# Attention and mixture-of-experts layer on one core: first-stage pairs, late rankings and the last output step moved in a slot schedule

## What is computed

```python
x = x + _layernorm(_L0_attn_ref(_layernorm(x), Wq, Wk, Wv, Wo))
x = x + _layernorm(_L0_ffn_ref(_layernorm(x), router_weight, router_bias, gate_up_proj, ...))

score = einsum('bhnd,bhmd->bhnm', q, k) / sqrt(16)      # causal mask, softmax
out = einsum('bhnm,bhmd->bhnd', softmax(score), v)      # then times Wo

topk_w, topk_idx = top_k(softmax(flat @ router_weight.T + router_bias), 2)
gu = flat @ gate_up_proj[e] + gate_up_bias[e]           # 512 gate and 512 up columns
act = (clip(up) + 1) * gate * sigmoid(1.702 * gate)
down = act @ down_proj[e] + down_bias[e]                # summed over the 2 experts by topk_w
```

## Time and profile before

| | us |
|---|---|
| median of three executions | 2084.46 (2081.51 to 2085.91) |
| the profiled execution's own time | 2083.6 |
| its span, first to last instruction | 2081.9 |

### The profile page before, as it was taken

One profiled execution on the slowest core, in us unless ns is written; L12 is line 12 of the kernel. 1 busy time (PEld: TensorE's weight loads), 2 busy tenths in 40 slices (PEclk: granted clock), 3 DMA queues, 4 the chain that ended last, 5 costly groups with the idle time before them and its releaser, 6 DMA issues.

```text
span 2081.9 us, 50245 instructions
## 1 busy us (share of the span) xinstructions
PE 1954.1 (94%) x13588; PEld 1296.6 (62%) x13589; DVE 1587.8 (76%) x5419; ACT 1335.3 (64%) x3405; POOL 939.8 (45%) x1437
## 2 busy tenths in 40 slices
PE   6799999999999999999999889999999999999990
PEld 4344444444444444444433338999999999999990
DVE  2877788888888888888788836778777777777777
ACT  3377777777777777777777675555445454544446
POOL 5233344455655646556454554554333333333336
PEclk9799999999999999999999999999999999999995
DMA  7633546465454554644536457978988899998778
GB/s 209 190 113 121 180 142 206 149 181 182 141 177 145 164 164 140 191 130 153 167 120 208 132 175 226 263 226 242 272 255 260 262 264 261 263 258 256 231 225 326
DMA packets 259188, 414.81 MB, mean 199 GB/s; under 512 B 37040, under 2 KB 194992, under 8 KB 251824
## 3 DMA queue, kind: packets, MB, share of 16 engines
q1 hardware_dynamic: 219520, 368.19, 54.5%
q0 software_dynamic: 29680, 35.41, 9.6%
q10 hardware_dynamic: 9792, 8.93, 1.4%
HBM read 289.55 MB, written 122.28 MB: 198 GB/s over the span
## 4 chain that ended last, share of the span: by engine, by line
PE 84%; DVE 9%; issue 4%; ACT 1%; DMA 1%; SPq 1%; DVEq 1%; POOL 0%; ACTq 0%; POOLq 0%
PE ps_s L1469 17%; PE ps_o L1353 13%; PE ps_s L1315 12%; PE ps_e L1334 11%; PE ps_e L1469 6%; PE ps_o L1486 5%; PE ps_e L1486 5%; PE ps_w L1385 5%; PE ps_w L1400 3%; PE ps_w L1416 3%; DVE arena L747 2%; PE ps_e L1479 1%; DVE cmax L750 1%; PE ps_w L1440 1%; DVE space L127 1%
## 5 line engine op out<-in xcount | busy, mean ns | idle before, releaser
L1113 ACT ACTIVATE arena<-ps_e 128x512 f32<-128x512 f32 (+3 forms) x1536 | 687.2, 493 | 275.8 <-PE ps_e L1334 266.7
L747 DVE CUSTOM_DVE_ANT_0 arena<-ps_s,c 128x128 bf16<-128x128 f32 (+3 forms) x1024 | 479.2, 481 | 60.3 <-PE ps_s L1315 56.4
L1315 PE MATMUL ps_s<-arena 96*128 96x512 bf16 (+3 forms) x1536 | 488.5, 333 | 25.6 <-DMA arena<-qk_parts 7.1
L1334 PE MATMUL ps_e<-arena 98*128 98x512 bf16 (+3 forms) x1536 | 483.5, 329 | 3.0 <-ACT arena L1113 2.8
L750 DVE TENSOR_REDUCE cmax<-ps_s 128x1 f32<-128x512 f32 x512 | 351.3, 686 | 142.4 <-PE ps_s L1315 138.9
L1315 PEld LDWEIGHTS ps_s<-arena 96*128 96x128 bf16 x1536 | 151.8, 100 | 355.7 <-DVE cmax L747 91.7
L1353 PE MATMUL ps_o<-arena 128*32 128x512 f32 (+3 forms) x3072 | 329.3, 501 | 6.6 <-ACT ot L1127 3.5
L643 POOL TENSOR_SCALAR_AFFINE_SELECT arena<-arena 128x512 f32<-128x512 f32 x256 | 163.2, 637 | 295.4 <-ACT arena L1113 295.1
L627 POOL DMA_INDIRECT acc<-blank,place_now x135 | 215.5, 1596 | 129.6 <-POOL place_now L622 70.6
L1469 PE MATMUL ps_s<-arena 128*128 128x128 f32 x2192 | 269.4, 276 | 0.0
L1469 PEld LDWEIGHTS ps_s<-arena 128*128 128x128 f32 x2192 | 263.4, 193 | 5.5 <-ACT arena L1255 0.6
(11 more groups left out here) (184 smaller groups left out, 3045.0 us busy)
## 6 DMA issues: line engine op xcount, KB each, us to landing
arena<-in_gate_up SPq DMA_DIRECT2D x93, 1024.0 KB, 6.1
arena<-qk_parts SPq DMA_DIRECT2D x384, 128.0 KB, 2.9
c_h<-in_gate_up SPq DMA_DIRECT2D x46, 1024.0 KB
qk_parts<-space SPq DMA_DIRECT2D x120, 192.0 KB, 3.2
d_xin<-xs SPq DMA_DIRECT2D x140, 130.5 KB, 3.2
v_aug<-space SPq DMA_DIRECT2D x32, 512.0 KB, 4.9
arena<-v_aug SPq DMA_DIRECT2D x32, 512.0 KB, 5.1
o_t<-ot SPq DMA_DIRECT2D x64, 256.0 KB, 2.0
```

Source lines behind the costliest of these rows:

```text
L747: dve.tensor_tensor_reduce(summed[:, m % RJ, 0:w], ps_s[:, m % RS, 0:w], after[:, HALF - w:HALF], 1.0, LOWEST, ALU.add, ALU.max, dst).then ...
L1113: act.activation(pw[:, n % RP, 0:w], ps_e[:, n % RE, 0:w], ACT.Exp, scale=SCALE).then_inc(e_done, 1)
L1315: pe.matmul(ps_s[:, m % RS, 0:w], qs[0:ROWS, slot, i * P:(i + 1) * P], ks[0:ROWS, slot, k0:k0 + w], start=True, stop=True).then_inc(s_scor ...
L1334: pe.matmul(ps_e[:, n % RE, 0:w], ks[0:ROWS_M, slot, j * P:(j + 1) * P], qs[0:ROWS_M, slot, q0:q0 + w], start=True, stop=True).then_inc(e_ ...
```

## The change

- **Pairs.** `A_AT` and `V_AT` of pairs 0 to 5 are four slots earlier. All six keep their places to one another, and move against the heads and against SyncE's block at `BEGIN`. SyncE's stores of pairs 4 and 5 stay behind that block. The load of pair 7's rows moves into the block, behind the value stores.
- **Value buffers.** Pairs 2 to 5 get buffers of their own (`vout_of`), in parts of `arena` that are not yet in use. VectorE sets them to one with four memsets of 128x1024. ScalarE no longer waits for a value store there, but waits at slot -1 for the stores of pairs 0 to 5.
- **Rows of -1.** One memset of 2x12288 becomes three of 2x4096, the first two slots ahead of `BEGIN`, the others six and nine slots behind it.
- **Second products.** From pair 6 on the second half of the query products, `q_or_k(a, 0, (2, 3))`, stands at part 3 of slot `A_AT + 1` instead of part 1 of `A_AT + 2`; its `first_part` and `remainder` go from parts 2 and 3 to parts 0 and 1 of that slot.
- **Ranks and scatters.** For groups 7 to 9 `rank`, `place`, the scatters and the late table stand one slot later. Scatters 2 to 7 of group 6 go four slots later, from slots 380 to 385 into 384 to 389.
- **Last step.** Step 15 is added and stored in two halves, the first as soon as two of its four normalising instructions are done.

```diff
-    A_AT = [BEGIN - 18 + 3 * a for a in range(EARLY)] + [BEGIN - 5, BEGIN + 2] + [NE * (a - 6) - 4 for a in range(6, PAIRS)]
-    V_AT = [BEGIN - 4 + a for a in range(EARLY)] + [start + 6 for start in A_AT[EARLY:]]
+    A_AT = [BEGIN - 22 + 3 * a for a in range(EARLY)] + [BEGIN - 9, BEGIN - 2] + [NE * (a - 6) - 4 for a in range(6, PAIRS)]
+    V_AT = [BEGIN - 8 + a for a in range(EARLY)] + [start + 6 for start in A_AT[EARLY:]]
...
-    S_AT = [G_AT[n] + (30 + k if n == B - 3 else EVEN[k] if n in STEADY else 27 + k) for n, k in SCATTERS]
-    LATE_TABLE_AT = G_AT[-1] + 27
+    S_AT = [G_AT[n] + (30 + k if n == B - 3 else EVEN[k] if n in STEADY else 27 + (n > B - 2) + (k + 4 if n == B - 2 and k > 1 else k)) for n, k in SCATTERS]
+    LATE_TABLE_AT = G_AT[-1] + 28
...
+        def vout_of(a):
+            if 2 <= a < EARLY:
+                at = 13312 + (a - 2) * 1024
+            elif EARLY <= a < EARLY + 2:
+                at = 16384 + (6, 10)[a - EARLY] * HALF
+            else:
+                return vout[:, a % 2]
+            return arena[:, at:at + 1024].rearrange("p (s c h d) -> p s c h d", s=4, c=2, h=4)
...
-                if g == BEGIN:
-                    pool.wait_ge(a_p3, 2 * EARLY + 1)
-                    pool.memset(ks[ROWS:ROWS_M], -1.0).then_inc(ones, 1)
-                    pool.wait_ge(ones, 1)
+                for u, (at, done_by, n) in enumerate(((BEGIN - 2, a_p3, 2 * EARLY + 2), (BEGIN + 6, a_p3, 2 * EARLY + 4), (BEGIN + 9, s_mlo, 2))):
+                    if g == at:
+                        pool.wait_ge(done_by, n)
+                        pool.memset(ks[ROWS:ROWS_M, u * 4:u * 4 + 4], -1.0).then_inc(ones, 1)
+                        pool.wait_ge(ones, u + 1)
...
+                for a in due((BEGIN - 18, BEGIN - 16, BEGIN - 14, BEGIN - 12), 0, g):
+                    dve.memset(vout_of(a + 2), 1.0).then_inc(v_ones, 1)
...
-                            if a >= 2:
+                            if 2 <= a < EARLY + 2:
+                                act.wait_ge(v_ones, a)
+                            if a >= EARLY + 2:
                                 act.wait_ge(v_out[u], a // 2 * 16)
...
-                        for n in groups_due(NEVER, 23, g):
+                        for n in groups_due(NEVER, 23, g, 1):
                             rank(n)
+                    if s == 3:
+                        for a in due(A_AT[FIRST_EVEN:], 1, g):
+                            q_or_k(FIRST_EVEN + a, 0, (2, 3))
...
-        for n in range(SHARED, STEPS):
+        for n in range(SHARED, STEPS - 1):
             dve.wait_ge(normed_ready, n + 1)
             dve.tensor_tensor(moe_of(n), moe_of(n), x1[:, n * NB:(n + 1) * NB], ALU.add).then_inc(added_last, 1)
+        n = STEPS - 1
+        for c in (0, 2):
+            dve.wait_ge(normed_ready, n + 1 + c // 2)
+            dve.tensor_tensor(moe_of(n)[:, c:c + 2], moe_of(n)[:, c:c + 2], x1[:, n * NB + c:n * NB + c + 2], ALU.add).then_inc(added_last, 1)
```

More of the change, by code:

```diff
@@ L113, in normalise @@
                 last = act.activation(moe_of(n)[:, c], moe_of(n)[:, c], ACT.Identity, scale=rstd[:, n, c:c + 1], bias=shift[:, n, c:c + 1])
+                if n == STEPS - 1 and c == 1:
+                    last.then_inc(normed_ready, 1)
             last.then_inc(normed_ready, 1)
@@ L191, in attention_layer, with groups_due @@
     MOMENTS = [(r, k) for slot, k, r in sorted((C_AT[r] + 3 + 6 * k, k, r) for r in range(PAIRS) for k in range(2))]
-    def groups_due(steady, late, slot):
-        return [n for n, start in enumerate(G_AT) if start + (steady if n in STEADY else late) == slot]
+    def groups_due(steady, late, slot, slack=0):
+        return [n for n, start in enumerate(G_AT) if start + (steady if n in STEADY else late + slack * (n > B - 2)) == slot]
     def rows_due(steady, quick, late, slot):
@@ L475, in _ @@
                     load_weights(n + WX, n % WX, later=(n + WX >= BESIDE))
-                for a in pairs_due(7, 9, g):
+                for a in due([max(start + (7 if a < FIRST_EVEN else 9), BEGIN + 1 if a >= EARLY else SLOTS.start) for a, start in enumerate(A_AT)], 0, g):
                     u, b, j = a % 2, a // PER, a % PER
@@ L483, in _ @@
                         store_values(a)
-                for a in pairs_due(-1, -9, g):
+                for a in due([SLOTS.start - 1 if a == 5 else start - (1 if a < FIRST_EVEN else 9) for a, start in enumerate(A_AT)], 0, g):
                     if EARLY <= a + 2 < PAIRS:
@@ L494, in _ @@
                         store_values(a)
+                    sp.wait_ge(a_xn, 6)
+                    sp.dma_start(ax[:, 1], x_v[7]).then_inc(ax_in[1], 16)
                     for early in range(1, SETS):
@@ L996, in _ @@
                             choose(n, 1)
+                        for a in due(A_AT[FIRST_EVEN:], 2, g):
+                            remainder(FIRST_EVEN + a, 0)
                         for n in groups_due(27, NEVER, g):
@@ L1034, in _ @@
                             choose(n, 2)
-                        for n in groups_due(27, 24, g):
+                        for n in groups_due(27, 24, g, 1):
                             place(n, 1)
-                        for n in groups_due(28, 25, g):
+                        for n in groups_due(28, 25, g, 1):
                             place(n, 2)
-                        for n in groups_due(29, 26, g):
+                        for n in groups_due(29, 26, g, 1):
                             place(n, 3)
                     if s == 3:
-                        for n in groups_due(NEVER, 23, g):
+                        for n in groups_due(NEVER, 23, g, 1):
                             place(n, 0)
-                        for a in due(A_AT, 2, g):
+                        for a in due(A_AT[0:FIRST_EVEN], 2, g):
                             remainder(a, 0)
@@ L1173, in _ @@
                 quad, c = divmod(g, NE)
+                if g == -1:
+                    for u in range(2):
+                        act.wait_ge(v_out[u], (EARLY + 2) // 2 * 16)
                 for s in range(4):
@@ L1179, in _ @@
                         high(head - 1)
+                    if s == 0:
+                        for a in due(A_AT[FIRST_EVEN:], 2, g):
+                            first_part(FIRST_EVEN + a, 0)
                     if s == 1:
@@ L1206, in _ @@
                             for t in range(2):
-                                last = act.activation(vout[:, u, :, t, :, 0:DH],
+                                last = act.activation(vout_of(a)[:, :, t, :, 0:DH],
                                                       bank[:, t * D:(t + 1) * D].rearrange("p (s h d) -> p s h d", s=4, h=4), ACT.Copy)
@@ L1492, in _ @@
                 if g == -1:
[L1493 removed]
+                    pe.wait_ge(ones, SETS)
                     pe.wait_ge(a_vout, EARLY)
```

12 lines of the change are left out of this document (8 added, 4 removed).

## The result

The changed kernel takes 2100.44 us (median of four, 2099.38 to 2101.64) against 2084.38 before: ratio 1.0077, 95% interval 1.0062 to 1.0092. It is 16 us slower. The forecast was 2072.9, faster, with a range of 2069.5 to 2079: wrong in sign.

What follows compares the result with a forecast made beforehand. Bound taken: TensorE's order of work among heads and first tiles, VectorE's chain of maxima ahead of the first exponential scores. Gains 5.5 - 0.1 + 0 + 4.2 + 0.8 + 1.2 = 11.6 us from 2083.6, plus 0.9: 2072.9, range 2069.5 to 2079.

Steps and rivals of the forecast that it cites:

- Second products: Query products moved sooner in 26 pairs among the heads: 0 us, bounds 0.1 us a pair either way (2.6 us).
- The sign of being wrong that the prediction named: Among the heads: the prediction is wrong if the quads change in length by more than 0.1 us each.
- The slower rival: In every quad TensorE waits for a score bank behind the sooner remainder, up to 0.61 us times 26: 2088.8; chance 0.05.
- First scores, the start: Ahead of the first exponential scores: the first maximum starts at 52.1 instead of 54.86, gain 2.8 us.
- First scores, the heads: Heads ahead of the first exponential scores: gains of 0.9, 0.6 and 1.4 us in heads 0 to 2, taken as 2.7.
- The clock: First heads: the first fall to half rate may not come; half rate may start sooner, at 0.2 us a head.
- the rival, half rate from the first head on: First heads stay as long as they are, 2.8 us gained instead of 5.5: 2076.4; chance 0.18.
- Memsets: Ahead of and among the first heads: 0.1 us for the buffers' four, 0 for the -1 rows, at worst 3.4 each.
- Ranks: At the ranks of groups 7 and 8: both TensorE waits go, 4.2 us, plus 0.8 for the clock.
- The rival that the waits move on: At the ranks: a wait of the same size comes at `place` and the bank's next user: 2077.9; chance 0.12.
- Last step: At the kernel's end: 0.6 us from the halved addition and 0.6 from the smaller store; together 1.2, bounds 0.6 and 1.9.

Runs made afterwards that it cites:

- run 3: The changed kernel with the second query products still sooner, but their first part and remainder (pairs 6 to 31) back at their old slot: 2089.97 us.
- run 4: The kernel half_product_sooner: 2082.93 us.
- Run 6: The kernel of run 3 with the plain maxima of slot 10 taken over 64 of 512 columns in quads 0 to 24: 2081.60 us.
- Run 8: The kernel of Run 6 with the steady groups' first step of choosing the experts moved behind the maxima of slot 10: 2075.97 us.
- run 5: The changed kernel, order kept, with the first remainder of pairs 6 to 31 computed for only 16 of 256 columns of each half: 2091.49 us.
- undo_second: The changed kernel with the second query products, first part and remainder of pairs 6 to 31 back at their old slots: 2074.34 us, ratio to before 0.9956.
- half_product_sooner: The kernel of run 3 with the second of the product's two weight steps also back at its old place: 2082.93 us.
- small_maxima_home: The kernel undo_second with the plain maxima of slot 10 taken over 64 of 512 columns in quads 0 to 24: 2073.85 us.
- Run 11: The kernel before with only the later ranks, scatters and late table of the change: 2076.09 us, ratio 0.9969.
- values_later: The kernel undo_second with the first half of the value products of pairs 6 to 31 at part 3 of their slot instead of part 1: 2083.86 us.

## Why the prediction was wrong

**Second products: the step that failed.** The prediction put them at 0 with bounds of 0.1 us a pair either way, because no instruction is added and because what TensorE's only steady wait of size hangs on does not move. It costs 24.5 us, 0.98 for each of the 25 pairs whose products stand in the stretch. Of this 16.7 come from the product's place (runs 3, 4, 6, 8), 3.5 of them by way of the stretched `diff`, and 7.8 from the remainder's (runs 3, 5). The sign of being wrong that the prediction named, quads that change by more than 0.1 us each, came. The mistake was to read the absence of a wait as room. TensorE had no wait on a maximum in slot 10 because 0.9 us of product stood between the second and third tile; VectorE's two idle times there, 0.58 and 0.41, were all the slack, and they belong to this arrangement. With 0.87 us taken from between the tiles, VectorE's chain is the limit, and it starts later too. Run 6 shows it: with a shorter chain the 0.53 us a quad fall to 0.06.

**The slower rival** had the remainder's half of this with 16 us and a chance of 0.05, and was argued away by "no wait of TensorE on a maximum repeats by quad now". That sentence is true of the trace and says nothing about the trace after the product has left. Its place was right; its price per pair (0.61 at most) was too high for the remainder (0.31) and left the product out (0.67).

**First scores, the start**: 52.1 forecast, 51.98 measured; the mechanism with the value buffers holds (gain 2.9).

**First scores, the heads**: 2.7 forecast, nothing there: 43.07 us from first maximum to first exponential scores instead of 42.54. This is a second step that failed, and a smaller one: "Head 1 loses its remainder: 6.3". Pair 5's eight value products move into head 1, wait 1.13 us for the pair's last remainder, and I had left them out. Head 1 took 9.24 us, and 7.96 in the two runs in which the clock did not fall there, so 1.7 us of it are theirs at full rate. Head 0 took 7.2 (forecast 7.8), head 2 6.55 (6.5). In all the stage gives 2.4 us here, 3.8 in undo_second.

**The clock**: head 0 kept full rate, as forecast (1.00 over 52 to 60 us), and the rival, half rate from the first head on, did not come. The Trainium skill, TensorE: Matmul & The Clock Gate, section HAM oscillation, which the prediction named for that rival, has gaps between bursts of matmuls bring the throttled clock back; the trace does not agree for head 0 and does for head 1. In one other execution it came in part: in half_product_sooner the clock was 0.79 over 54 to 57 us and head 0 took 8.32 instead of 7.22. The clock fell behind the 1.13 us wait in head 1 (0.57 in 60 to 64), came back (1.00 in 64 to 68), and was 0.51 from 70 to 90, as the text had said for the heads from 2 on.

**Memsets**: the two later ones, 3.51 us each on GpSimd, ended at 70.20 and 76.30 and held up the next difference by 1.4 and 1.0 us; behind them head 2 was as short as forecast, and head 3 with 7.57 was 0.4 longer than its 7.2. In small_maxima_home, with the same memsets, head 3 took 7.21, so it is not shown that the 0.4 is theirs. Nearly right.

**Ranks**: the waits are gone (4.2), no new one came, and the clock stayed at 1.00 behind group 8. Run 11 gives 6.4, the trace 6.2: with all of the 1.6 us of the clock stretch, not half, the sum would have been 5.8. The rival that the waits move on did not come.

**Last step**: ScalarE's last eight instructions start at 2089.93 and the span ends 7.8 us later, instead of 8.3. The halved addition gives its 0.6; the smaller store lands after 2.6 us like the large one, so that part gives 0, the lower bound.

```profile
2089.93 4.04 ACT L118 ACTIVATE space<-space 128x256 f32<-128x256 f32 x8
...
2093.18 1.51 DVE L161 TENSOR_TENSOR space<-space,arena 128x512 f32<-128x512 f32 x2
```

The terms without the second products sum to 9 us as measured, against 11.6 forecast.

**Open**: what lets the clock fall behind a wait in one execution and not in another (below). Stages with the same order also differ by 1 to 2 us ahead of the first exponential scores and in the last heads; how much of that is the clock is not shown.

## What to carry to other kernels

In an order written out by hand, a wait that is absent tells of the order as it stands. Before moving a piece of the fuller engine out of a stretch, work through the other engine's queue in that stretch: here 0.61 + 0.31 + 0.61 + 0.59 + 0.13 = 2.25 us of VectorE behind the slot's first tile, three banks between the engines, and 0.9 us of product whose absence makes that the limit.

Here work that feeds no one cost least when spread between pieces that feed the next engine. Two fillers in a row starve it for 1.45 us, and the tiles behind them then come too fast; with half of the product back between the tiles, 0.43 of the 0.53 us a quad were won back.

A short wait in a full slot (0.45 us at the values) can be cheaper than the move that removes it.

Two numbers that agree with a theory in sum can hide two others. The half product's 8.0 of 16.7 us looked like one half; by quad it was a fifth in 20 quads, and in five a longer `diff` stood in for what was won back.

## What the runs showed of the hardware

**VectorE and GpSimd on a short subtraction.** `diff`, 128x64 with both inputs and its output in SBUF, takes 0.21 us in before and undo_second. It takes 0.68 in the changed kernel and 1.12 in half_product_sooner; in both it starts while GpSimd adds 128x512 (1.26 us), and the earlier in that addition it starts, the longer it takes. From the timeline of the changed kernel:

```profile
424.51 1.26 POOL L715 TENSOR_TENSOR x_sb<-c_y,c_x 128x512 f32<-128x512 f32 x1
...
425.17 0.68 DVE L805 TENSOR_TENSOR diff<-top 128x64 f32<-128x64 f32 x1
```

It ends at 425.85, 0.08 behind GpSimd's end at 425.77. The Trainium skill, SBUF — State Buffer, section Who interferes with whom, says that a VectorE instruction with two SBUF inputs contends with a GpSimd one that reads SBUF; the trace agrees, with 0.2 us becoming up to 1.2. Run 8, where the subtraction stands elsewhere, shows the cost of such a hit in front of the maxima: 1.1 us a quad. It is not the addition alone. In small_maxima_home `diff` starts with GpSimd's cut of the diagonal tiles and takes 0.62 us:

```profile
414.46 0.63 POOL L666 TENSOR_SCALAR_AFFINE_SELECT arena<-arena 128x512 f32<-128x512 f32 x1 [2.65 <-ACT arena L1140]
414.55 0.62 DVE L807 TENSOR_TENSOR diff<-top 128x64 f32<-128x64 f32 x1
```

There the quads stay at 955.8 us: with the product between the tiles the hit costs nothing.

**The clock is not decided by the order alone.** In head 1 the same wait of 1.12 to 1.13 us stands in undo_second and in small_maxima_home, which have the same program there. In the first the clock fell (0.79 over 58 to 66) and the four products took 1.99 us; in the second it stayed at 1.00 and they took 1.13. From the timeline of TensorE, undo_second:

```profile
59.34 1.99 PE L1430 MATMUL ps_w<-space 128*128 128x256 f32 x4 [1.13 <-DVE space L793]
```

small_maxima_home:

```profile
59.56 1.13 PE L1432 MATMUL ps_w<-space 128*128 128x256 f32 x4 [1.12 <-DVE space L795]
```

The head took 9.24 and 7.96 us. Of ten runs with this wait two (the other is values_later) kept 1.00 over 58 to 66 us. So a term that rests on the clock falling or not behind one wait carries 1.3 us of chance in one execution.
